# Merging the seven loads of a row's turned one-hots into one transfer in the mask stage of a graph network kernel

## The chip, the cores and the metric

The kernel runs on one core of one Trainium2 chip. The metric is device time in microseconds (us) of the whole program. Engines are TensorE (PE), VectorE (DVE), ScalarE (ACT), GpSimd (POOL) and SyncE (SP), which here only issues DMA transfers.

## What is computed

A graph network on 6,250 nodes with 64 features and 200,000 edges. The first layer adds up neighbours; the second makes three hops, in each of which every edge gets a mask from a small network of its two ends, and the messages are summed with these masks.

```python
def _L0_gnn_ref(feat, src, dst, n_nodes):
    return jax.ops.segment_sum(feat[src], dst, num_segments=n_nodes)

def _L1_gnn_ref(features, nb_W, nb_b, self_W, self_b, att1_W, att1_b, att2_W, att2_b, row, col):
    x = out = features
    for l in range(3):
        f1 = jax.nn.relu(x[row] @ nb_W[l] + nb_b[l])
        f2 = jax.nn.relu(x[col] @ self_W[l] + self_b[l])
        h = jax.nn.relu(jnp.concatenate([f1, f2], axis=1) @ att1_W[l] + att1_b[l])
        log_alpha = (h @ att2_W[l] + att2_b[l])[:, 0]
        mask = jnp.clip(jax.nn.sigmoid(log_alpha) * (1.05 + 0.45) - 0.45, 0.0, 1.0)
        rowsum = jax.ops.segment_sum(mask, row, num_segments=n) + 1e-06
        d_inv_sqrt = jnp.clip(rowsum ** (-0.5), 0.0, 10.0)
        vals = mask * d_inv_sqrt[row] * d_inv_sqrt[col]
        x = jax.ops.segment_sum(vals[:, None] * x[col], row, num_segments=n)
        out = out + x
    return out

h = relu(layernorm(x));  x = x + _L0_gnn_ref(h, src, dst, 6250)
h = relu(layernorm(x));  x = x + _L1_gnn_ref(h, ..., src, dst)
```

## The kernel before

The nodes are padded to 49 blocks of 128. The edges are sorted once into 49 x 49 bins, one for each pair of a source block and a destination block, with up to 128 edges in each. For every bin a stage called `build_and_sum` makes one-hot matrices of 128 x 128 bytes: the source one-hot turned, the destination one-hot turned, and the source one-hot as it is. They are written to `hot_scratch` in device memory, laid out as [49 rows, 128 partitions, 7 groups, 3 kinds, 7 x 128]. A "row of bins" is the 49 bins of one source block; it is worked on in NG = 7 groups of G = 7 bins.

After that, three layers run in a hardware loop. Each layer has small matrix products (`node_products`), the mask stage (`edge_masks`), the row scales (`scale_rows`) and the message stage (`sum_messages`). Both large stages read the one-hots back from `hot_scratch`, row by row.

The change lies in the mask stage. `each_row` runs row 0 unrolled and then 24 turns of a hardware loop with two rows in each (the odd row in buffer 1, the even row in buffer 0), so each buffer is used by every second row. In a row:

- SP loads `hotT_a`, the two turned one-hots, line 1089, in seven transfers of 128 x 1792 bytes (224 KB), and then `hot_a`, the unturned one, line 1091, in one transfer of 128 x 7 x 896 bytes (784 KB). Both are double buffered. Before piece g it waits until the gather of group g of the row two before is over (`gathered`), and before `hot_a` it waits until the mask sums of the row two before are over (`summed`).
- TensorE's `gather`, line 1110, makes 42 matmuls of 128x128 by 128x64 for each group: the turned source one-hot by `rows_a`, this row's node products, and the turned destination one-hot by `table`, each in three bf16 parts, into `pre_ps[g]`. Before group g it waits for piece g, and for VectorE to have emptied `pre_ps[g]` (`weigh`). After the gather of group 5 it runs `sum_masks` of the row before, line 1122, 49 matmuls of `hot_a` by `parts`, and then the gather of group 6.
- VectorE applies the relu and the attention weights (line 1190) and reduces to one logit for each edge (line 1177). ScalarE makes the sigmoid (line 1138) and copies the next row's `rows_a` (line 1144). GpSimd clips and splits the masks (lines 1156 to 1163).

The order on each engine is the order of the code; engines meet at semaphores alone. `wait_count` is a wait for a count held in a register, and it also bumps a counter (`hold_waits`, line 53).

## Time and profile before

| | us |
|---|---|
| median of 3 runs | 4841.93 |
| lowest and highest | 4841.65, 4844.85 |
| profiled execution | 4840.7 |
| its span, first to last instruction | 4839.1 |
| TensorE busy | 4293.3 (89%) |
| VectorE busy | 4118.9 (85%) |

The profile is of one execution. A row of the grouped instructions reads: line, engine, operation, output and inputs with shapes, how many, then busy time in us and mean ns of one, then the idle time of the engine just before them and what ended it. "issue" is time in which the engine waited for nothing that the profile shows. "Landing" is the time from the issue of a transfer to its last completion. The mask stages of the three layers run from about 1645 to 2155 us, 2723 to 3232 us and 3801 to 4310 us of the span.

### The profile page before, as it was taken

The numbers are of one execution on the slowest core, as the hardware profiler recorded it, in microseconds if no ns is written. First come the engines' busy times: TensorE is split into PE (matmuls) and PEld (weight loads), VectorE is DVE, ScalarE is ACT, GpSimd is POOL, SyncE is SP. The second block draws the span as 40 slices with busy tenths as digits, with TensorE's granted clock in tenths as the row PEclk, the third lists the DMA queues.
The fourth block names the chain that finished last, engine by engine and source line by source line (L and its number), as shares of the span: only waits on it lengthen the run. The fifth ranks groups of instructions, "written<-read, shape, count | busy, mean of one in ns | idle before, by whom it ended". The sixth has DMA issues, their size and how long they took to land. (4 is left out here: it accounts for less than half of the span.)

```text
span 4839.1 us, 255754 instructions
## 1 busy us (share of the span) xinstructions
PE 4293.3 (89%) x100368; PEld 4029.1 (83%) x100369; DVE 4118.9 (85%) x7921; ACT 2222.8 (46%) x3957; POOL 2223.9 (46%) x3431
## 2 busy tenths in 40 slices
PE   6888885999998699979999799979998899979998
PEld 5777774888887599978888699978888699978887
DVE  7677767999999588879999588879999588879998
ACT  0000002999999111117777211117777211127776
POOL 1222222777775222217777322227777222227776
PEclk7777776999999799989999899989999899989999
DMA  1000002888887277756665377756665477756664
GB/s 27 1 1 1 1 1 64 260 268 266 266 270 233 92 242 239 239 172 175 161 161 148 116 239 239 239 180 162 161 161 133 135 239 239 239 175 161 162 161 132
DMA packets 532160, 793.98 MB, mean 164 GB/s; under 512 B 66422, under 2 KB 466218, under 8 KB 532074
## 3 DMA queue, kind: packets, MB, share of 16 engines
q1 hardware_dynamic: 499146, 714.06, 46.8%
q0 software_dynamic: 32928, 78.72, 7.0%
q8 instruction: 60, 0.98, 0.1%
q14 instruction: 26, 0.21, 0.0%
HBM read 672.34 MB, written 120.23 MB: 164 GB/s over the span
## 5 line engine op out<-in xcount | busy, mean ns | idle before, releaser
L1110 PE MATMUL pre_ps<-rows_a,hotT_a 128*128 128x64 bf16 x21609 | 1285.5, 194 | 54.0 <-DMA hotT_a<-hot_scratch 27.3
L1339 POOL TENSOR_TENSOR message<-message,message_parts 128x448 f32<-128x448 f32 x1029 | 1100.8, 1070 | 438.4 <-ACT message_parts L1324 433.8
L1110 PE MATMUL pre_ps<-table,hotT_a 128*128 128x64 bf16 x21609 | 1286.5, 194 | 11.6 <-issue 11.6
L1110 PEld LDWEIGHTS pre_ps<-rows_a,hotT_a 128*128 128x128 fp8e4 x21609 | 1131.9, 99 | 68.1 <-issue 67.9
L1110 PEld LDWEIGHTS pre_ps<-table,hotT_a 128*128 128x128 fp8e4 x21609 | 1132.8, 99 | 5.7 <-issue 5.7
L1350 DVE TENSOR_TENSOR message_parts<-message,message_parts 128x448 bf16<-128x448 f32 x1029 | 942.3, 916 | 2.7 <-ACT message_parts L1315 2.7
L1190 DVE SCALAR_TENSOR_TENSOR weighed<-pre_ps,w 128x448 f32<-128x448 f32 x1029 | 642.4, 624 | 321.3 <-PE pre_ps L1110 229.1
L1277 PE MATMUL row_ps<-table,hot_b 128*128 128x64 bf16 x21609 | 801.3, 194 | 68.7 <-DMA hot_b<-hot_scratch 65.0
L1290 PE MATMUL sum_ps<-message_parts,hot_b 128*128 128x192 bf16 x7203 | 760.3, 245 | 90.1 <-DVE message_parts L1350 75.9
L1277 PEld LDWEIGHTS row_ps<-table,hot_b 128*128 128x128 fp8e4 x21609 | 754.9, 99 | 81.4 <-issue 81.4
L1324 ACT ACTIVATE message_parts<-message 128x448 bf16<-128x448 f32 x1029 | 593.6, 577 | 421.1 <-DVE message L1365 421.1
L1290 PEld LDWEIGHTS sum_ps<-message_parts,hot_b 128*128 128x128 fp8e4 x7203 | 556.1, 97 | 168.3 <-issue 107.1
L737 POOL DMA_DIRECT2D places<-slots_scratch x686 | 543.0, 793 | 239.0 <-issue 158.4
L1365 DVE TENSOR_TENSOR message<-row_ps,mask 128x448 f32<-128x448 f32 x1029 | 627.5, 610 | 17.0 <-PE row_ps L1277 16.7
L1177 DVE TENSOR_REDUCE logit<-weighed 128x7 f32<-128x448 f32 x1029 | 626.4, 609 | 0.0
L1138 ACT ACTIVATE gate<-logit,b 128x49 f32<-128x49 f32 x147 | 49.6, 337 | 1227.8 <-DVE logit L1177 1227.8
L1315 ACT ACTIVATE message_parts<-message 128x448 bf16<-128x448 f32 x1029 | 578.9, 563 | 1.5 <-POOL message L1339 1.3
L1158 POOL TENSOR_SCALAR fresh<-gate 128x49 f32<-128x49 f32 x147 | 35.1, 239 | 1126.9 <-ACT gate L1138 1126.9
L867 DVE TENSOR_SCALAR hot<-places,pcol 128x1792 uint8<-128x1792 uint8 x343 | 409.7, 1195 | 1.3 <-DMA places<-slots_scratch 1.2
L409 PE MATMUL bins_ps<-spread,value_w 128*98 128x128 bf16 x1764 | 317.5, 371 | 98.7 <-issue 50.5
L409 PEld LDWEIGHTS bins_ps<-spread,value_w 128*98 128x98 bf16 x1764 | 309.9, 268 | 109.4 <-issue 109.4
L831 ACT ACTIVATE hot<-src_ps 128x896 uint8<-128x896 f32 x343 | 369.3, 1077 | 43.4 <-PE src_ps L763 43.0
(145 smaller groups left out, 5554.9 us busy)
## 6 DMA issues: line engine op xcount, KB each, us to landing
hotT_a<-hot_scratch SPq DMA_DIRECT2D x1029, 224.0 KB, 4.6
hot_b<-hot_scratch SPq DMA_DIRECT2D x1029, 224.0 KB, 2.6
hot_scratch<-hot SPq DMA_DIRECT2D x343, 336.0 KB, 5.6
hot_a<-hot_scratch SPq DMA_DIRECT2D x147, 784.0 KB, 5.1
places<-slots_scratch POOLq DMA_DIRECT2D x686, 112.0 KB, 5.3
out<-res SPq DMA_DIRECT2D x1, 1536.0 KB
slots_scratch<-bins SPq DMA_DIRECT2D x49, 12.2 KB
raw<-in_src SPq DMA_DIRECT2D x1, 768.0 KB
```

The lines of the kernel that those rows point to most:

```text
L409: last = nc.tensor.matmul(bins_ps[b][:, :], value[:, b, :, w], spread[:, w, :], start=w == 0, stop=w == WIN - 1)
L737: pool.dma_start(places[:, g, e, :], tile.rearrange("r c e -> (r c e)").partition_broadcast(P))\
L1110: last = nc.tensor.matmul(pre_ps[g][:, j, :], hotT[:, b, g, end, j * P:(j + 1) * P].bitcast(FP8), table, start=end + part == 0, stop=end = ...
L1177: dve.tensor_reduce(logit[:, b, g * G:(g + 1) * G], weighed[:, (b + g) % 2, :, :], X, ALU.add)\
L1190: dve.scalar_tensor_tensor(weighed[:, (b + g) % 2, :, :], pre_ps[g][:, 0:G, :], 0.0, k.w3[:, :].unsqueeze(1).to_broadcast([P, G, D]), ALU. ...
L1277: last = nc.tensor.matmul(row_ps[g % 4][:, j, :], hot[:, b, g, 0, j * P:(j + 1) * P].bitcast(FP8), k.table_d[:, g * G + j, part, :], start ...
L1290: last = nc.tensor.matmul(sum_ps[b][:, :], hot[:, b, g, 1, j * P:(j + 1) * P].bitcast(FP8), parts[:, g, j, :, :].rearrange("p c d -> p (c ...
L1315: nc.scalar.activation(parts[:, g, :, 1, :], message[:, g, :, :], ACT.Copy)\
L1324: nc.scalar.activation(parts[:, g, :, 0, :], message[:, g, :, :], ACT.Copy)\
L1339: pool.tensor_tensor(message[:, g, :, :], message[:, g, :, :], parts[:, g, :, 0, :], ALU.subtract).then_inc(s["rest_ready"], 1)
L1350: dve.tensor_tensor(parts[:, g, :, 2, :], message[:, g, :, :], parts[:, g, :, 1, :], ALU.subtract).then_inc(s["third_ready"], 1)
L1365: dve.tensor_tensor(message[:, g, :, :], row_ps[g % 4][:, 0:G, :], k.mask[:, bass.ds(r * NB + g * G, G)].unsqueeze(2).to_broadcast([P, G, D]),
```

## The change

In the mask stage the seven transfers of `hotT_a` for a row become one transfer of 128 x 7 x 1792 bytes (1,568 KB), with one semaphore for each of the two buffers in place of seven. SP waits before it for all seven gathers of the row two before, and TensorE waits for it before the first gather of a row only.

```diff
-        sems = " ".join([f"in{b}_{g}" for b in range(2) for g in range(NG)] + ["src_in0", "src_in1"])
+        sems = "in0 in1 src_in0 src_in1"
...
-            loaded = [[s[f"in{b}_{g}"] for g in range(NG)] for b in range(2)]
+            loaded = [s["in0"], s["in1"]]
...
                     tiles = k.hot_dram[bass.ds(r, 1), :, :, :, :].rearrange("r p g a b -> (r p) g a b")
-                    for g in range(NG):
-                        if not first:
-
-                            wait_count(sp, s, s["gathered"], (r - 1) * NG + g + 1)
-                        sp.dma_start(hotT[:, b, g, :, :], tiles[:, g, 0:2, :]).then_inc(loaded[b][g], 16)
+                    if not first:
+                        wait_count(sp, s, s["gathered"], r * NG)
+                    sp.dma_start(hotT[:, b, :, :, :], tiles[:, :, 0:2, :]).then_inc(loaded[b], 16)
                     wait_count(sp, s, s["summed"], r + 1)
                     sp.dma_start(hot[:, b, :, :], tiles[:, :, 2, :]).then_inc(src_loaded[b], 16)
...
                 def gather(q, r, g, b, nth):
-                    pe.wait_ge(loaded[b][g], nth * 16)
+                    if g == 0:
+                        pe.wait_ge(loaded[b], nth * 16)
                     pe.wait_ge(s["weigh"], q + 1)
```

`gathered` starts at NG, so the value r * NG is reached when group 6 of row r - 2 is done.

SP's order in the loop's second row (even rows, buffer 0), with the wait for `gathered` on a register instruction and the DMA behind it. Before:

```order
L1091 DMA hot_a<-hot_scratch 128x7x896
L58 ISA
L1089 REGISTER_ALU [waits gathered]
L1089 DMA hotT_a<-hot_scratch 128x1792
L58 REGISTER_ALU
...
L1089 DMA hotT_a<-hot_scratch 128x1792
L58 REGISTER_ALU
L1091 REGISTER_ALU [waits summed]
L1091 DMA hot_a<-hot_scratch 128x7x896
```

The same place after (the file is one or two lines shorter, so line numbers move):

```order
L1089 DMA hot_a<-hot_scratch 128x7x896
L58 REGISTER_ALU
L1087 REGISTER_ALU [waits gathered]
L1087 DMA hotT_a<-hot_scratch 128x7x1792
L58 REGISTER_ALU
L1089 REGISTER_ALU [waits summed]
L1089 DMA hot_a<-hot_scratch 128x7x896
L102 REGISTER_ALU
```

Between the same two `hot_a` transfers, seven pairs of a wait and a transfer have become one pair.

TensorE's order at the head of the loop, where the first gather of an odd row begins. Before:

```order
L102 UNCONDITIONAL_BRANCH
L102 ISA
L1101 ISA [waits in1_0]
L1103 REGISTER_ALU [waits weigh]
L1110 MATMUL pre_ps<-rows_a,hotT_a 128x64 [waits rows_ready]
```

After:

```order
L102 UNCONDITIONAL_BRANCH
L102 ISA
L1100 ISA [waits in1]
L1102 REGISTER_ALU [waits weigh]
L1109 MATMUL pre_ps<-rows_a,hotT_a 128x64 [waits rows_ready]
```

The instructions are the same; the wait is for the whole row's transfer in place of its first piece. The order of VectorE, ScalarE and GpSimd is unchanged.

## Rows read from the trace of the kernel before

**Rows 1.** The page's part 1: busy us and share of each engine.

```profile
PE 4293.3 (89%) x100368; PEld 4029.1 (83%) x100369; DVE 4118.9 (85%) x7921; ACT 2222.8 (46%) x3957; POOL 2223.9 (46%) x3431
```

**Rows 2.** The page's part 5, then the list of waits: mask stage's gather.

```profile
L1110 PE MATMUL pre_ps<-table,hotT_a 128*128 128x64 bf16 x21609 | 1286.5, 194 | 11.6 <-issue 11.6
L1110 PE MATMUL pre_ps<-rows_a,hotT_a 128*128 128x64 bf16 x21609 | 1285.5, 194 | 54.0 <-DMA hotT_a<-hot_scratch 27.3 <-issue 26.7
...
PE pre_ps L1110 <- DMA hotT_a<-hot_scratch: 27.3, 3, 9.1
```

**Rows 3.** Busy time by window, mid-stage in the second layer; columns in the first line.

```profile
core 0: us, PE busy (x) PEld busy (x) DVE busy (x) ACT busy (x) POOL busy (x), PEclk, DMA share, GB/s
2750.00:3220.00 470.00, 461.58 (x16005) 459.31 (x16002) 378.30 (x700) 88.99 (x139) 101.05 (x373) 1.00 0.71 238
```

**Rows 4.** Timeline (start us, us, what) of TensorE where three successive rows begin.

```profile
1727.54 0.22 PE L1110 MATMUL pre_ps<-rows_a,hotT_a 128*128 128x64 bf16 x2 [0.28 <-issue]
...
1737.35 0.25 PE L1110 MATMUL pre_ps<-rows_a,hotT_a 128*128 128x64 bf16 x3
...
1747.55 0.25 PE L1110 MATMUL pre_ps<-rows_a,hotT_a 128*128 128x64 bf16 x3 [0.24 <-issue]
```

**Rows 5.** Timeline of SP's issues in one row of bins.

```profile
1726.24 0.56 SPq L1091 DMA_DIRECT2D hot_a<-hot_scratch  x1
1727.16 4.16 SPq L1089 DMA_DIRECT2D hotT_a<-hot_scratch  x7
```

**Rows 6.** The seventh of these pieces: its issue, and us to landing.

```profile
L1089 SPq DMA_DIRECT2D hotT_a<-hot_scratch x1: 333/333/333, 1731.0 to 1731.0; - x1
...
DMA to landing us min/median/max: 4.4/4.4/4.4
```

**Rows 7.** Us to landing of hot_a, 44 issues of steady rows, first layer.

```profile
DMA to landing us min/median/max: 4.8/5.1/5.4
```

**Rows 8.** By window (columns as in rows 3), one steady row of bins.

```profile
1727.00:1728.00 1.00, 0.72 (x26) 0.63 (x22) 0.70 (x2) 0.00 (x0) 0.00 (x0) 1.00 0.27 27
1728.00:1729.00 1.00, 1.00 (x41) 1.00 (x38) 0.55 (x3) 0.00 (x0) 0.00 (x0) 1.00 0.74 220
1729.00:1730.00 1.00, 1.00 (x41) 1.00 (x38) 1.00 (x2) 0.00 (x0) 0.00 (x0) 1.00 1.07 375
...
1734.00:1735.00 1.00, 1.00 (x42) 1.00 (x38) 0.94 (x2) 0.00 (x0) 0.00 (x0) 1.00 0.71 258
```

**Rows 9.** Timeline: the first issue and TensorE's first matmul, first layer.

```profile
1644.59 3.19 SPq L1089 DMA_DIRECT2D hotT_a<-hot_scratch  x7
...
1647.31 0.27 PE L1110 MATMUL pre_ps<-rows_a,hotT_a 128*128 128x64 bf16 x2 [9.12 <-DMA hotT_a<-hot_scratch]
```

**Rows 10.** First seven pieces, layers one and two: issues, and us to landing.

```profile
L1089 SPq DMA_DIRECT2D hotT_a<-hot_scratch x7: 345/433/435, 1644.6 to 1647.3; - x7
...
DMA to landing us min/median/max: 2.6/4.1/4.7
...
L1089 SPq DMA_DIRECT2D hotT_a<-hot_scratch x7: 342/428/435, 2722.7 to 2725.5; - x7
...
DMA to landing us min/median/max: 2.5/3.9/5.1
```

**Rows 11.** By window (columns as in rows 3), the first layer's start.

```profile
1647.00:1648.00 1.00, 0.69 (x14) 0.72 (x15) 0.00 (x0) 0.96 (x1) 0.00 (x0) 0.50 0.87 186
1648.00:1652.00 4.00, 4.00 (x80) 4.00 (x78) 0.64 (x2) 0.00 (x0) 0.00 (x0) 0.51 0.98 339
```

**Rows 12.** Timeline of TensorE at the loop's first entry in each layer.

```profile
1660.43 0.25 PE L1110 MATMUL pre_ps<-rows_a,hotT_a 128*128 128x64 bf16 x3 [2.31 <-issue]
...
2738.57 0.25 PE L1110 MATMUL pre_ps<-rows_a,hotT_a 128*128 128x64 bf16 x3 [2.03 <-issue]
...
3818.48 0.25 PE L1110 MATMUL pre_ps<-rows_a,hotT_a 128*128 128x64 bf16 x3 [2.85 <-issue]
```

**Rows 13.** By window (columns as in rows 3), behind the third of these.

```profile
3819.00:3823.00 4.00, 4.00 (x90) 4.00 (x87) 1.73 (x4) 0.59 (x2) 1.06 (x4) 0.57 0.47 169
```

## The prediction

> **What bounds the kernel now.** Read the page's first part before anything else: TensorE has matmuls under way for 89% of the span [rows 1]. Then the grouped instructions: the mask stage's gather, line 1110, holds 2,572 us of that as two groups of 21,609 matmuls, and the whole idle time before them is 65.6 us, of which 27.3 us is put down to the transfers that the change merges [rows 2]. The list of waits says where those 27.3 us lie: three waits, the longest 9.1 us [rows 2]. There are three layers, so each wait is the first gather of a layer's mask stage, when nothing is loaded yet. In all the other 144 rows of bins the gather never waits for a transfer.
>
> Next the steady part of the stage. Over 470 us in the middle of the second layer's stage TensorE is busy 461.6 us at full clock, VectorE 378.3, and the DMA engines 71% [rows 3]. Two rows of bins, from one return of the loop to the next, take 1747.55 - 1727.54 = 20.0 us, so 10.0 us each [rows 4]. What TensorE waits for at the return is "issue", 0.24 to 0.28 us, not data. So the stage is TensorE's, and a transfer matters only if it lands after the gather that reads it could begin.
>
> **Steady state: what is given up and what hides it.** The order of SP's instructions shows three edits: seven transfers of 224 KB become one of 1,568 KB; it waits for the end of the last gather of the row two before, where the first of the seven waited for that row's first gather; and the gather's later six groups have no wait for data. In fact SP stands in front of the `summed` wait until the mask sums of the row before, which come after group 5, so the seven are issued late already. In the trace the 784 KB of `hot_a` go out at 1726.24 and the seven at 1727.16 and after [rows 5]. The new wait ends when group 6 ends. The first matmul of the next row starts at 1727.54 after a pause of 0.28 us [rows 4], so group 6 was over at about 1727.26, and the merged transfer is issued at about 1727.3 to 1727.4: 0.2 us later than the first piece. It is issued 3.6 us earlier than the seventh piece, which goes out at 1731.0 and lands 4.4 us later, at 1735.4 [rows 6].
>
> All this data is for the row that begins at 1737.35, 9.8 us after 1727.54 [rows 4]. The merged transfer stands behind `hot_a`, which lands some 5.1 us after its issue [rows 5, 7], at 1731.3. From 1729 on the engines move 375 GB/s, and in the last us before 1735 they run out of work (258 GB/s, share 0.71) [rows 8]: they are full of work and the issue is not what holds them. So the bytes end where they ended. I take a landing at 1735.4 + 0.2 = 1735.6 and a margin of 1.8 us. **Steady cost: 0.** TensorE was not held by the waits that vanish either: they ride on register instructions that the sequencer still runs, since the order keeps their number, and both `pre_ps` groups together show only 38.3 us of "issue" in 147 rows [rows 2]. I take 0 for them. If the cover were gone, each us beyond it would cost half a us a row, because the merged transfer for one row starts at the end of the row two before: two rows would then last the transfer plus one row.
>
> A page of the Trainium skill speaks for the change at this place: "DMA: Bandwidth & Descriptors", Measured, asks for transfers of at least 1 MiB to reach 75% of peak. The trace doesn't bear it out for this queue: 224 KB pieces queued back to back already move 375 GB/s [rows 8], and by that rule too the steady term would be 0, since the bytes are hidden.
>
> **The start of each layer: the term that decides.** Here there is no cover. In the first layer SP issues the first piece at 1644.59 and TensorE starts at 1647.31, having waited 9.12 us [rows 9]. The piece took 2.6 us, 2.5 in the second layer [rows 10]. Afterwards TensorE needs all seven pieces. When is the whole there?
> - Upper bound, from the seven pieces as they are. The seventh goes out at 1647.3 and the longest of the seven takes 4.7 us: 1652.0, or 7.4 us after the first issue. In the second layer 2725.5 + 5.1 - 2722.7 = 7.9 us [rows 10].
> - Lower bound: the first piece's 2.6 us, and then six more at the steady pace. 1,568 KB are 1.606 MB, which at 375 GB/s [rows 8] take 4.3 us, or 0.6 us a piece: 2.6 + 3.6 = 6.2 us.
> - Nearest row for a single large transfer: `hot_a`, 784 KB, one DMA of the same form on the same queue, idle before it: 4.8 to 5.4 us, median 5.1 [rows 7]. The second 784 KB add 2.1 us at 375 GB/s: 7.2 us.
>
> The seven pieces have a dip on the way, 186 GB/s from 1647 to 1648 [rows 11], which a single transfer may or may not show. I take 7.0 us. TensorE then starts 7.0 - 2.6 = 4.4 us later in each layer, and three layers make **+13.2 us**, with 3 x 3.6 = 10.8 and 3 x 5.3 = 15.9 as ends. Nothing later gives it back: the stage is TensorE's, so its end moves by what its start moves. The first row's matmuls run at half clock, level 1.2 GHz, from 1647.31 until almost 1652 (granted clock 0.50, then 0.51 as a mean to 1652) [rows 11], and VectorE, ScalarE and GpSimd wait for them.
>
> The page "DMA: Bandwidth & Descriptors", Anatomy of one DMA, gives a fit made on another issuing path, 2.0 us plus bytes over 436 GB/s. As an estimate it makes the whole 5.7 us and the piece 2.5 us, so 3.2 us a layer and 9.5 us in all; the trace agrees on the piece (2.6 us) and not on the rate (375 GB/s) [rows 8, 10].
>
> **What comes back in the next few rows of bins.** At the first entry into the loop TensorE stands still for "issue": 2.31, 2.03 and 2.85 us before its first matmul [rows 12]. With the start later, the four transfers of the first two rows, 4.8 MB or 12.8 us at 375 GB/s, are through when the first row ends, some 7.0 + 10.8 us after the first issue. If all three waits fell to the shortest, 1.1 us would come back. In the third layer the longest of them is followed by four us at a mean clock of 0.57 [rows 13], so 3.4 us at half clock, which cost 1.7 us; I give that an even chance to go, 0.8 us. How long the half clock lasts after a later start is not in the trace; I take no change, and a us a layer either way for the range. Sum: **-1.9 us**, between -5 and +2. The saving on SP, six issues of 0.33 us a row, lies on a queue that next waits for TensorE's mask sums, from 1731.3 to the next `hot_a`, so 0. The reset of twelve fewer semaphores at the stage's end is one instruction as before: 0.
>
> **The sum.** 13.2 - 1.9 = +11.3 us. The profiled execution took 4840.7 us around a span of 4839.1, so it becomes 4852.0. The median of the runs is 1.2 us above it, 4841.9, which gives **4853.2 us**, 0.23% slower. About 0.2%, 9.7 us, is what a measurement of this kernel can tell from no change, so the forecast lies just beyond the line.
>
> **Rivals.**
> 1. *The large transfer flows without the dip.* The whole lands 6.2 us after issue, the start costs 10.8 us, and the loop entries give back 4 or 5: +6 us, 4848 us, not slower by the bound. For it: the seven pieces pay seven issues of some 0.43 us each [rows 10], and a single DMA pays one. Against it: `hot_a`, which is a single DMA, needs 5.1 us for half the bytes [rows 7]. It decides below 6.5 us for the whole: 3 x (6.5 - 2.6) - 1.9 = 9.8. The skill's fit above falls on this side: 9.5 - 1.9 = +8 us.
> 2. *The cover in the steady state is too thin.* The place is each row's first gather. If the merged transfer needed twice `hot_a`'s time, 10.2 us from 1727.4, it would land at 1737.6, 0.25 us after its row should start. Half of that a row, by the chain above, is 144 x 0.125 = 18 us, with the 11.3 about 4871 us. Against it: `hot_a`'s 5.1 us has a slow first us (27 GB/s, then 220) [rows 8] that isn't repeated behind a full queue. It decides from a landing 1.8 us later than I take.
> 3. *Something shortens the steady row.* If the 0.26 us of "issue" at the loop's return fell away, 23 returns in each of three layers would give 18 us: 11.3 - 18 = -7, 4835 us; with the start and the loop entries at their low ends too, 10.8 - 5 - 18 = -12, 4830 us, which would count as faster. Against it: the instructions at the loop's head are the same ones in the same order, and the wait that stands there stays.
>
> **How the numbers follow.** Forecast as summed, whole transfer 6.5 to 8 us: 0.57. Rival 1: 0.32. Rival 2: 0.07. Rival 3: 0.04. The range reaches from rival 1's low end, 10.8 - 5 - 1, to the forecast's high end, 15.9 + 2: 4846.5 to 4860. It leaves out rivals 2 and 3 and a little of the tails. Slower by over 0.2%: 0.57 + 0.07, less a little where the loop entries give back more than I take, 0.60. Within 0.2%: 0.37. Faster: 0.03.
>
> **What would show it.** Right: the wait for `hotT_a` at the start of each layer grows from 9.1 to some 13.5 us, the three waits together from 27.3 to 40; the first issue to the landing is about 7 us; two steady rows still take 20.0 us; no later gather waits for `hotT_a`. Wrong: waits for `hotT_a` counted by the hundred (rival 2), waits at the start under 13.0 us each (rival 1), or a steady pair of rows that isn't 20.0 us. A changed count or length of half-clock stretches in the first 40 us of a layer would move the sum by 1 to 2 us each.

## The result, and the profile after

| | before, us | after, us |
|---|---|---|
| median of 9 runs | 4841.65 | 4856.64 |
| lowest and highest | 4838.1, 4845.56 | 4851.9, 4863.34 |
| span of the profiled execution | 4839.1 | 4855.0 |
| TensorE busy | 4293.3 | 4294.9 |

The changed kernel is slower by 0.31%: ratio 1.0031, 95% interval 1.0021 to 1.0042, or 15 us with an interval of 10 to 20. The forecast was 4853.2 us in a range of 4846.5 to 4860. TensorE's busy time has grown by no more than 1.6 us, so nearly all of the loss is idle time between its matmuls.

The first view is the page of the changed kernel, parts 1, 5 and 6, with the lines that answer to [rows 1, 2], and from the list of waits the line on `hotT_a`:

```profile
PE 4294.9 (88%) x100368; PEld 4028.2 (83%) x100369; DVE 4120.0 (85%) x7921; ACT 2222.7 (46%) x3957; POOL 2227.7 (46%) x3431
...
L1109 PE MATMUL pre_ps<-rows_a,hotT_a 128*128 128x64 bf16 x21609 | 1286.7, 193 | 66.9 <-DMA hotT_a<-hot_scratch 43.7
...
hotT_a<-hot_scratch SPq DMA_DIRECT2D x147, 1568.0 KB, 9.0
...
PE pre_ps L1109 <- DMA hotT_a<-hot_scratch: 43.7, 8, 14.2
```

The waits for `hotT_a` grew from 27.3 us in three waits to 43.7 us in eight. Three of them are the starts of the layers. In the timeline of TensorE, kernel after, they are these, against 9.12 us in [rows 9]:

```profile
1648.89 0.26 PE L1109 MATMUL pre_ps<-rows_a,hotT_a 128*128 128x64 bf16 x2 [14.16 <-DMA hotT_a<-hot_scratch]
...
2734.31 0.27 PE L1109 MATMUL pre_ps<-rows_a,hotT_a 128*128 128x64 bf16 x2 [13.68 <-DMA hotT_a<-hot_scratch]
...
3819.66 0.26 PE L1109 MATMUL pre_ps<-rows_a,hotT_a 128*128 128x64 bf16 x2 [13.57 <-DMA hotT_a<-hot_scratch]
```

They add up to 41.4 us. The other five waits hold the remaining 2.3 us. The first is the transfer itself. SP's issues at the first layer's start, and the answer for the tile `hotT_a` there, kernel after:

```profile
1641.14 0.62 SPq L1087 DMA_DIRECT2D hotT_a<-hot_scratch  x1
1641.82 0.65 SPq L1089 DMA_DIRECT2D hot_a<-hot_scratch  x1
...
L1087 SPq DMA_DIRECT2D hotT_a<-hot_scratch x1: 624/624/624, 1641.1 to 1641.1; - x1
...
DMA to landing us min/median/max: 7.6/7.6/7.6
```

The whole of a row lands 7.6 us after its issue, where 7.0 was assumed, and TensorE starts 1648.89 - 1641.14 = 7.75 us after the issue. Before it was 2.72 us [rows 9].

Next the steady rows. SP's issues in the row that [rows 5] shows, the landing of the transfer issued at 1727.29, and the landings of 43 issues in the middle of the first layer's stage:

```profile
1726.05 0.54 SPq L1089 DMA_DIRECT2D hot_a<-hot_scratch  x1
1727.29 0.54 SPq L1087 DMA_DIRECT2D hotT_a<-hot_scratch  x1
...
DMA to landing us min/median/max: 9.0/9.0/9.0
...
L1087 SPq DMA_DIRECT2D hotT_a<-hot_scratch x43: 542/543/570, 1707.2 to 2128.9; - x43
...
DMA to landing us min/median/max: 8.5/8.9/10.0
```

And TensorE's rows of bins, as in [rows 4]:

```profile
1727.35 0.22 PE L1109 MATMUL pre_ps<-rows_a,hotT_a 128*128 128x64 bf16 x2 [0.28 <-issue]
...
1737.15 0.22 PE L1109 MATMUL pre_ps<-rows_a,hotT_a 128*128 128x64 bf16 x2
...
1747.36 0.22 PE L1109 MATMUL pre_ps<-rows_a,hotT_a 128*128 128x64 bf16 x2 [0.23 <-issue]
```

A pair of rows still takes 1747.36 - 1727.35 = 20.0 us. But the data for the row that starts at 1737.15 landed at 1727.29 + 9.0 = 1736.3, only 0.86 us before it, where the prediction had 1.8 us. The landings scatter from 8.5 to 10.0 us, so some come too late. Over the 138 rows from row 3 on in the three layers, worked out from the single landings, the median time from the last landing to the row's first matmul is 1.84 us before and 0.83 us after.

Where did the bytes lose time? Busy time by window in that row (columns as in [rows 3]); the last two figures of a line are the DMA share and GB/s:

```profile
1729.00:1730.00 1.00, 1.00 (x41) 1.00 (x37) 0.92 (x2) 0.04 (x1) 0.00 (x0) 1.00 1.06 371
1730.00:1731.00 1.00, 1.00 (x41) 1.00 (x38) 0.95 (x2) 0.55 (x2) 0.43 (x2) 1.00 0.91 275
...
1734.00:1735.00 1.00, 1.00 (x42) 1.00 (x39) 1.00 (x2) 0.00 (x0) 0.00 (x0) 1.00 0.68 256
1735.00:1736.00 1.00, 1.00 (x46) 1.00 (x43) 0.88 (x3) 0.00 (x0) 0.00 (x0) 1.00 0.15 56
```

There is a dip to 275 GB/s from 1730 to 1731, and a thin tail, 56 GB/s from 1735 to 1736. The completions of the single transfer explain the tail: it is done when the last of the 16 DMA engines is, and in the trace their completions lie between 1734.67 and 1736.29, 1.6 us apart. Those of the seventh piece before lay between 1734.95 and 1735.42, 0.5 us apart. Over the same 138 rows the median spread is 1.7 us after (0.8 to 3.3) and 0.7 us for the seventh piece before (0.4 to 2.4).

### The profile page after: what moved, and what is told of

Read it like the earlier page. It is cut to its first block and busy times, and to the rows that moved or that the text cites. A ratio compares the mean times of both kernels' runs of the same rounds, so it can differ in the third digit from the quotient of the medians.

```text
span 4855.0 us, 251416 instructions
## 1 busy us (share of the span) xinstructions
PE 4294.9 (88%) x100368; PEld 4028.2 (83%) x100369; DVE 4120.0 (85%) x7921; ACT 2222.7 (46%) x3957; POOL 2227.7 (46%) x3431
## 5 line engine op out<-in xcount | busy, mean ns | idle before, releaser
L1109 PE MATMUL pre_ps<-rows_a,hotT_a 128*128 128x64 bf16 x21609 | 1286.7, 193 | 66.9 <-DMA hotT_a<-hot_scratch 43.7
L1109 PE MATMUL pre_ps<-table,hotT_a 128*128 128x64 bf16 x21609 | 1287.8, 193 | 11.7 <-issue 11.7
L409 PEld LDWEIGHTS bins_ps<-spread,value_w 128*98 128x98 bf16 x1764 | 309.9, 268 | 111.4 <-issue 111.4
```

The lines of the kernel that those rows point to most:

```text
L409: last = nc.tensor.matmul(bins_ps[b][:, :], value[:, b, :, w], spread[:, w, :], start=w == 0, stop=w == WIN - 1)
L1109: last = nc.tensor.matmul(pre_ps[g][:, j, :], hotT[:, b, g, end, j * P:(j + 1) * P].bitcast(FP8), table, start=end + part == 0, stop=end = ...
```

## Where the 15.9 us of the two spans went

The table is worked out from the starts of single matmuls in the two traces; the stretches of the three layers are added up. "Start" is from the first issue of `hotT_a` to the first gather matmul. A row of bins lasts from its first gather matmul to the next row's first. Rows 3 to 47 are split into those that end inside the loop's turn (69) and those that end at its return (66).

| stretch, us | before | after | difference |
|---|---|---|---|
| start | 8.10 | 22.18 | +14.1 |
| rows 0 to 2 | 117.6 | 114.1 | -3.5 |
| rows 3 to 47, ending inside the turn | 676.5 | 678.5 | +2.0 |
| rows 3 to 47, ending at the return | 675.7 | 677.6 | +1.9 |
| until the first issue, and from one layer's messages to the next layer's first issue | 1754.7 | 1757.2 | +2.5 |
| message stage and the rest | | | -1.0 |

In this bookkeeping of one execution the start is nearly the whole difference, as predicted, and three other terms are of 2.5 to 4 us each, with different signs. That it would go if the start alone were undone doesn't follow; the experiments below test it. The +2.5 is itself the sum of two differences: the first issue comes 3.5 us earlier after than before, and the two stretches between layers are 6.0 us longer together.

**The first rows are shorter, above all at the loop's first entry.** In the timeline of TensorE, kernel after, the rows that answer to [rows 12] are:

```profile
1660.76 0.22 PE L1109 MATMUL pre_ps<-rows_a,hotT_a 128*128 128x64 bf16 x2
...
2745.81 0.22 PE L1109 MATMUL pre_ps<-rows_a,hotT_a 128*128 128x64 bf16 x2
...
3831.47 0.19 PE L1109 MATMUL pre_ps<-rows_a,hotT_a 128*128 128x64 bf16 x1 [0.39 <-issue]
```

Waits of 2.31, 2.03 and 2.85 us for "issue" have become 0.39 us or less. In exchange there is a wait earlier, in row 0, and the one that row 2 had before is longer (from start to start of two matmuls 2.8, 3.4 and 2.8 us in the three layers, before 2.5, 2.5 and 1.7). The longest of each kind in TensorE's timeline, kernel after:

```profile
1656.80 0.26 PE L1109 MATMUL pre_ps<-rows_a,hotT_a 128*128 128x64 bf16 x3 [1.28 <-issue]
...
2765.46 0.21 PE L1109 MATMUL pre_ps<-table,hotT_a 128*128 128x64 bf16 x1 [3.16 <-issue]
```

The list of queues for the stretch of the second of these, 2762 to 2766, shows what else was moving:

```profile
DMA  7899889999999999998998989989765442322222
...
q1 hardware_dynamic: 690, 1.22, 82.1%
q8 instruction: 1, 0.02, 1.5%
```

In these four us there is one packet on the instruction queue, among 690 packets of the one-hots on engines that are some nine tenths busy for the first seven tenths of the stretch. My reading is that TensorE stands for its code behind data.

The start times of the single packets on that queue, 16 KB each, bear this out. At all 42 loop entries of the 14 profiles (those of the runs below included) the last such packet goes out 2.7 to 3.1 us before row 1's first matmul, whether TensorE idles 0.1 or 3.1 us there. What differs is how far it lies behind the packet ahead of it: 6.0, 5.5 and 6.4 us before, where TensorE idles 2.31, 2.03 and 2.85 us; 3.7, 3.5 and 3.9 us after, where it idles 0.11, 0.11 and 0.39. Over the 42 entries the idle time goes with that distance almost in step (correlation 0.99), and from row 5 to row 47 of each layer before there is no packet on that queue. What spaces the packets out is still an inference: no run here moved the code alone.

**A second half-clock stretch takes a part of it back.** The long waits of row 2 are followed by half clock in all three layers after, and not before. By window (columns as in [rows 3]), four us from the matmul that ends the longest wait of row 2, the three layers after, then the second layer before:

```profile
1679.85:1683.85 4.00, 4.00 (x87) 4.00 (x87) 2.02 (x4) 0.00 (x0) 0.00 (x0) 0.59 0.11 39
2765.46:2769.46 4.00, 4.00 (x90) 4.00 (x90) 2.03 (x4) 0.00 (x0) 0.00 (x0) 0.61 0.11 38
3850.02:3854.02 4.00, 4.00 (x85) 4.00 (x85) 2.30 (x4) 0.00 (x0) 0.00 (x0) 0.57 0.11 40
...
2758.49:2762.49 4.00, 3.96 (x137) 3.90 (x137) 3.18 (x6) 0.00 (x0) 0.00 (x0) 1.00 0.19 67
```

A mean of 0.57 to 0.61 over four us means 3.1 to 3.4 us at half clock (1.2 GHz), which do the work of half that time at full clock: an estimate of 1.6 to 1.7 us lost in each layer, some 5 us in all. Before, the only such stretch past row 0 is the one behind the third loop entry [rows 13]. In the second profile of the kernel after (below) row 2 has it in two of the layers (0.62 and 0.57).

**The stretch between the layers varies in length.** From the last message matmul of a layer to the first issue of the next layer's mask stage, by window, before and then after (the clock is third from the end):

```profile
2667.85:2722.71 54.86, 36.83 (x176) 22.27 (x174) 25.26 (x55) 16.35 (x27) 25.64 (x14) 0.79 0.03 4
...
2668.61:2727.04 58.43, 39.48 (x177) 23.62 (x174) 25.27 (x55) 16.34 (x27) 25.63 (x14) 0.77 0.02 4
```

The work is the same to within three records; VectorE, ScalarE and GpSimd are busy for the same time, and TensorE is busy for 2.7 us more at a lower mean granted clock. The change touches nothing there. In the profiles of before, after and the eight runs below that load row 0 within the mask stage, the 20 such stretches are of 54.9 to 58.7 us, nine of them under 56. Runs that merge all rows have short ones too (54.9 us in the second profile of the kernel after), but before was profiled once, with two short ones. I take these us for chance in a profile; that the change has no part in them is argued, not shown.

## Experiments

The claims to be told apart: the loss comes from the start, where TensorE waits for the whole instead of one piece; or it comes from the other 48 rows, where the cover is too thin; and, for the cause, the size of the transfer or the coarser wait. Runs with the same time of before in the table at the end ran on one chip, beside the same runs of before.

**Row 0 in pieces, the other rows merged.** Against the kernel after:

```diff
-                    if not first:
+                    if first:
+                        for g in range(NG):
+                            sp.dma_start(hotT[:, b, g, :, :], tiles[:, g, 0:2, :]).then_inc(pieces[g], 16)
+                    else:
                         wait_count(sp, s, s["gathered"], r * NG)
-                    sp.dma_start(hotT[:, b, :, :, :], tiles[:, :, 0:2, :]).then_inc(loaded[b], 16)
+                        sp.dma_start(hotT[:, b, :, :, :], tiles[:, :, 0:2, :]).then_inc(loaded[b], 16)
...
-                    if g == 0:
-                        pe.wait_ge(loaded[b], nth * 16)
+                    if first:
+                        pe.wait_ge(pieces[g], 16)
+                    elif g == 0:
+                        pe.wait_ge(loaded[b], nth * 16 if b == 1 else (nth - 1) * 16)
```

> The merged kernel with one part undone: the first row of each layer is loaded in seven pieces again, each with its own wait; the 144 other rows keep the merged transfer and its single wait. Theory (the start is the whole cost): TensorE starts 2.7 us after the first issue in each layer instead of 7.2 to 7.8, so 5.0 + 4.6 + 4.4 = 14 us go, and the kernel lands within 0.1% of the kernel before, 4840 to 4846 us. Rival (the merged transfer costs in the steady rows, where it lands 9.0 us after its issue with some 0.8 us to spare): no more than half of the 15 us goes, 4849 us or more.

Measured: 4862.94 us, ratio 1.0041 (1.0027 to 1.0055). The start is back at 8.1 us for the three layers, and yet the kernel is 21.6 us slower than before. The trace says that 9.0 us stand in the rows that end at the loop's return: median 10.36 us each, where before has 10.25 and after 10.21. Another 8.9 us stand in rows 0 to 2 (126.5 us against 117.6). Here are two loop returns of this kernel; the idle time is 0.39 us against 0.24 to 0.28 in [rows 4]:

```profile
1727.37 0.22 PE L1115 MATMUL pre_ps<-rows_a,hotT_a 128*128 128x64 bf16 x2 [0.39 <-issue]
...
1747.53 0.19 PE L1115 MATMUL pre_ps<-rows_a,hotT_a 128*128 128x64 bf16 x1 [0.39 <-issue]
```

The count `(nth - 1) * 16` was mine and no part of the change. So the run doesn't answer its question.

**Seven transfers, one wait.** Against after:

```diff
-                    sp.dma_start(hotT[:, b, :, :, :], tiles[:, :, 0:2, :]).then_inc(loaded[b], 16)
+                    for g in range(NG):
+                        sp.dma_start(hotT[:, b, g, :, :], tiles[:, g, 0:2, :]).then_inc(loaded[b], 16)
...
-                        pe.wait_ge(loaded[b], nth * 16)
+                        pe.wait_ge(loaded[b], nth * (16 * NG))
```

> Waits as in the merged kernel (one for the whole row, SP after the last gather, TensorE before the first), but seven transfers of 224 KB in place of one of 1,568 KB, on one semaphore for each buffer. Theory (it is the coarser wait, not the size of the transfer, that costs): the start is as late as the seventh piece of the kernel before, 7.4 to 7.9 us after the first issue, so the time stays at 4853 to 4860 us. Rival (a large transfer is itself slower to land): the start is nearer 6.2 us and the time 4850 or less. On the steady landing: issued from 1727.3 on at 0.64 us each, the seventh piece goes out 3.8 us later and lands 4.4 us after that, 8.2 us after the first issue, against 9.0 us for the one transfer; if the size is what makes the landing late, the occasional late rows (five waits beside the three starts) vanish.

Measured: 4856.45 us, ratio 1.0032 (1.0021 to 1.0043). The changed count costs here too (median 10.34 us at the return, 6.6 us in all), so the total says little. The parts of the trace say more. In the list of waits of this kernel:

```profile
PE pre_ps L1110 <- DMA hotT_a<-hot_scratch: 43.0, 3, 14.6
```

Three waits, all at starts, which take 8.19, 8.10 and 7.48 us from the first issue: as late as with the single transfer (7.75, 7.27, 7.16). It is the wait for the whole that costs at the start, not the size of the transfer. No later row waits for `hotT_a`. In rows 3 to 48 the last of the seven pieces lands a median 8.0 us after the first issue, where the single transfer takes 9.0, and 1.92 us before its row begins (after: 0.83). The longer returns, 0.13 us each, don't explain that, so it is the size that makes the steady landings late.

**Row 0 merged, the others in seven.** Against before:

```diff
-                    for g in range(NG):
-                        if not first:
-
+                    if first:
+                        sp.dma_start(hotT[:, b, :, :, :], tiles[:, :, 0:2, :]).then_inc(s["row0_in"], 16)
+                    else:
+                        for g in range(NG):
                             wait_count(sp, s, s["gathered"], (r - 1) * NG + g + 1)
-                        sp.dma_start(hotT[:, b, g, :, :], tiles[:, g, 0:2, :]).then_inc(loaded[b][g], 16)
+                            sp.dma_start(hotT[:, b, g, :, :], tiles[:, g, 0:2, :]).then_inc(loaded[b][g], 16)
...
-                    pe.wait_ge(loaded[b][g], nth * 16)
+                    if not first:
+                        pe.wait_ge(loaded[b][g], nth * 16 if b == 1 else (nth - 1) * 16)
+                    elif g == 0:
+                        pe.wait_ge(s["row0_in"], 16)
```

> The kernel before with one part of the change alone: row 0 of each layer is loaded in one transfer with one wait, all other rows keep seven pieces with seven waits. Theory (start alone): +13 to +15 us, 4854 to 4857 us, and no wait for hotT_a beside the three at the starts. Rival (steady rows pay part of it): under +8 us.

Measured: 4859.42 us, ratio 1.0037 (1.0024 to 1.0051), with 8.0 us more than before in the rows at the loop's return (median 10.36 us). Confounded in the same way.

**Row 0 loaded a stage earlier, the others in seven.** Against before; `hotT_a` is allocated over both stages, and the stage ahead loads row 0 into it behind its weights and waits for it at its end:

```diff
+                sp.dma_start(k.hotT[:, 0, :, :, :],
+                             k.hot_dram[0:1, :, :, 0:2, :].rearrange("r p g a b -> (r p) g a b")).then_inc(s["row0_in"], 16)
+                sp.wait_ge(s["row0_in"], 16)
...
-                    pe.wait_ge(loaded[b][g], nth * 16)
+                    if not first:
+                        pe.wait_ge(loaded[b][g], nth * 16 if b == 1 else (nth - 1) * 16)
```

> The kernel before, with row 0's 1,568 KB loaded during the small matrix products ahead of the mask stage, one transfer behind the weights, so that the first gather waits for no transfer. Theory (the path at a layer's start runs through the issue and landing of row 0): TensorE starts some 2.4 us earlier in each layer, bounded below by ScalarE's copy of rows_a, which ends at 1646.7 against TensorE's start at 1647.3; so at least 0.6 x 3 = 2 us and at most 7 us faster, 4835 to 4840 us. Rival (the transfer disturbs the matrix products or their weight loads): no gain or a loss of a few us.

Measured: 4840.73 us, ratio 1.0001 (0.9992 to 1.001). Of the gain at the start 9.6 us go to the loop's return (685.36 us against 675.72).

**The same with the counts left alone.** The four following runs keep `nth * 16` as it is. Where row 0 is loaded apart, SP adds the 16 itself, as in this piece of the first of them:

```diff
                     if first:
                         for g in range(NG):
                             sp.dma_start(hotT[:, b, g, :, :], tiles[:, g, 0:2, :]).then_inc(pieces[g], 16)
+                        sp.sem_inc(loaded[b], 16)
...
-                        pe.wait_ge(loaded[b], nth * 16 if b == 1 else (nth - 1) * 16)
+                        pe.wait_ge(loaded[b], nth * 16)
```

Row 0 in pieces, the others merged:

> Row 0 in seven pieces and all other rows merged, as in the first form of this experiment, which landed at 4862.9 us. In that form the wait of the even rows compared with a changed count, and the trace shows 0.15 us more at each of the 69 returns of the loop, 10 us in all. Here SyncE adds the missing 16 to the merged semaphore itself, so TensorE's loop is the same as in the merged kernel. Theory (the start is the cost, the head of the loop was the disturbance): the returns take 10.21 us a row again, the start 2.7 us a layer, and the time is 4840 to 4848 us. Rival (pieces first and merged transfers after slow down the first three rows of a layer, 126.5 us there against 114.1 merged): 4850 to 4856 us.

Measured: 4851.7 us, ratio 1.0026 (1.0017 to 1.0035): the rival's range, not the 4840 to 4848 of the theory. Row 0 merged, the others in seven:

> The kernel before with row 0 alone merged, in the same clean form (TensorE's loop as in the kernel before). Its first form came to 4859.4 us, of which the returns of the loop explain 8 us. Theory: the start costs 14 us, the first three rows give back 3 to 6, so 4849 to 4853 us, the returns 10.21 to 10.25 us. Rival (the head of the loop does not matter): 4857 or more again.

Measured: 4852.61 us, ratio 1.0024 (1.0015 to 1.0033). Row 0 a stage earlier, the others in seven:

> The kernel before with row 0 loaded during the small matrix products, TensorE's loop unchanged. The first form (a changed count in the even rows) took 4840.7 us with returns of 10.39 us in place of 10.25: 9 us lost there. Theory: those 9 us come back, 4830 to 4834 us, faster than the kernel before by 0.15 to 0.25%. Rival: no change, 4839 or more.

Measured: 4830.72 us, ratio 0.9981 (0.9972 to 0.999). Row 0 a stage earlier, the others merged:

> The merged kernel with row 0 loaded during the small matrix products, TensorE's loop unchanged. It takes the start away and leaves what the merged transfer costs in the other rows. Theory (start 22.2 us in three layers is the main cost, late rows 4 us the rest): 4836 to 4842 us, that is 2 to 8 us above the same kernel with seven pieces. Rival (the merged transfer costs nothing in the steady rows): equal to the kernel with seven pieces within 2 us.

Measured: 4847.19 us, ratio 1.0012 (1.0003 to 1.0021). Both expectations for this run are missed: 4836 to 4842 us, and within 2 us of the kernel above it. In all four the median row at the loop's return is back at 10.21 us. A loop return of the first of the four shows it:

```profile
1726.81 0.22 PE L1116 MATMUL pre_ps<-rows_a,hotT_a 128*128 128x64 bf16 x2 [0.23 <-issue]
```

That settles where the extra 9 us of the first runs came from. The instructions listed at the head of the loop are the same in both forms; in the trace the step from the loop's register operation to the wait is 0.37 us in the first form and 0.26 us in the kernel after. What the sequencer does in between isn't recorded.

Now the medians, each against the before of the same chip (4840.05 us):

| us | others in seven | others merged | difference |
|---|---|---|---|
| row 0 in pieces | 4840.05 (before) | 4851.7 | +11.7 |
| row 0 merged | 4852.61 | 4854.75 (another chip, before 4839.83) | +2.1 |
| row 0 a stage earlier | 4830.72 | 4847.19 | +16.5 |

The start alone costs 12.6 us. But merging the other 48 rows costs 12 to 16 us where the mask stage starts early, and about 2 us where it starts late. The two parts don't add: 12.6 + 11.7 would be 24.3, the change costs 15. Read the other way: each part alone costs most of the 15 us, and undoing one of them in the changed kernel gives back only 2 to 3 (4854.75 to 4852.61 or to 4851.7). The intervals are some 4 us wide to either side, so the sizes are rough, but the difference between +2.1 and +16.5 is beyond them.

The traces show part of the reason in rows 0 to 2 of the three layers: 117.6 us before, 112.1 with only row 0 merged, 111.4 in a second profile of the kernel after (114.1 in the first), but 120.8 with row 0 in pieces and the others merged, and 117.1 and 123.1 for the two that load row 0 early. With an early start these rows run beside 4.8 MB of transfers, and merged ones lengthen them by 3.2 (120.8 - 117.6) and 5.9 us (123.1 - 117.1); with a late start the queue is drained when the loop is entered, and they get shorter. Late steady rows add 0 to 7 us by the profiles: rows 3 to 47 are 0.4 us shorter than before in the first of the four, and 7.3 us longer in the last than in the third. That doesn't fill the 11.7 us of the first of the four. Its span is 8.5 us above before's, of which 3.2 lie in rows 0 to 2, and 6.5 ahead of and between the stages, where the kernels don't differ and the lengths vary in all of them. These parts are a guide only: the profiled execution of the first of the four took 4849.21 us against a median of 4851.7, and that of the last was the slowest of its eleven, 4853.61 against 4847.19. Why merging the other rows costs 12 to 16 us with an early start stays open.

**More bytes ahead of the merged transfer.** Against after, with one tile more; its data is read by nobody, so 448 KB a row (with `0:4` in place of `0:2`, 896 KB) are only load:

```diff
                     if not first:
                         wait_count(sp, s, s["gathered"], r * NG)
+                        wait_count(sp, s, more_in[b], nth * 16 if b == 1 else (nth - 1) * 16)
+                        sp.dma_start(more[:, b, :, :, :], tiles[:, 0:2, 0:2, :]).then_inc(more_in[b], 16)
```

> The merged kernel with 448 KB more loaded ahead of each row's merged transfer, into a buffer that nothing reads. It measures how thin the cover in the steady rows is. In the merged kernel's trace the transfer lands 8.9 us after its issue and the row that reads it starts 9.67 or 9.82 us after that issue, of which some 0.3 us pass between a landing and a first matmul that waited for it. Theory (0.4 to 0.6 us of cover, then half a us a row for each us beyond): the landing moves by 448 KB at 375 GB/s, 1.2 us, so 0.7 us too late and 0.35 us a row, 144 rows make 50 us on top of the merged kernel: 4890 to 4915 us, waits for hotT_a in over 100 rows. Rival (the cover is 1.8 us, as predicted): no change, 4860 us at most.

Measured: 4886.66 us, ratio 1.0095 (1.008 to 1.0111), 32 us above the unchanged merged kernel on the same chip, where 4890 to 4915 was expected.

> The same with 896 KB more, 2.4 us of transfer. Theory (half a us a row for each us beyond the cover): 1.9 us too late, 0.95 us a row, 137 us on top of the merged kernel, 4980 to 5010 us. Rival (every us beyond the cover costs a whole us a row, since each row has one transfer): some 270 us, 5100 us or more.

Measured: 5056.97 us (one run), 202 us above it, between the two ranges that were expected. The list of waits, first the kernel with 448 KB, then that with 896 KB:

```profile
PE pre_ps L1118 <- DMA hotT_a<-hot_scratch: 74.7, 45, 14.4
...
PE pre_ps L1118 <- DMA hotT_a<-hot_scratch: 178.7, 77, 14.3
```

The 8 waits of the kernel after have become 45, and then 77, which is about every second of the 144 rows: two rows share one late transfer, as the prediction's chain says. With 448 KB the waits grow by 31.0 us, which is about the loss of that run. These bytes would take 1.2 us at 375 GB/s (0.459 MB), but in the trace the landing moves by less: counted from the start of the row before, its median goes from 9.2 to 9.7 us. The engines move 315 GB/s from 1727 to 1737, where they moved 241 in the kernel after. So half a us more is already enough to use up the margin of many rows, which the prediction put at 1.8 us. With 896 KB the waits grow by 135 us, and the rest has another cause; the page's part 1 of that kernel:

```profile
PE 4368.9 (86%) x100368; PEld 4102.5 (81%) x100369; DVE 4119.9 (81%) x7921; ACT 2222.0 (44%) x3957; POOL 2220.9 (44%) x3431
```

TensorE, which now pauses in every second row, is busy for 74 us more with the same matmuls, and its mean granted clock over the span is 0.913 against 0.926. In rows 3 to 47 of its three mask stages the mean granted clock is 0.94 to 0.96, against 1.00 in the kernel after. In the second layer, for instance, the row that starts at 3006.56 behind a wait of 2.04 us lasts 11.36 us at a mean of 0.85, where a row without a pause takes 9.81. So these pauses cost themselves, and matmuls behind them run at a lower clock as well.

**The change once more.** The kernel after, on the chip of the last two and of the next.

> The merged kernel once more, unchanged, in the same stretch of chip time as the others, for a second profile of it. Theory: 4853 to 4860 us; the wait at the start of each layer 13.5 to 14.5 us; some late rows beside the three starts, though not the same ones. If the late rows do not come again, they were a chance of one execution.

Measured: 4854.75 us, ratio 1.0033 (1.0021 to 1.0045). Its trace has a start of 22.3 us and seven waits for `hotT_a`, 43.4 us; rows 3 to 47 are 1.5 us longer than before's (1.5 inside the turn, 0.0 at the return), where the first profile had 3.8. So the starts repeat, and the late rows are few and vary.

**Row 0 of both large stages a stage earlier.** Against before: as in the third of the four, and the same for `hot_b` of the message stage, loaded in `scale_rows`:

```diff
+        @block.sync
+        def _(sp):
+            sp.dma_start(k.hotB[:, 0, :, :, :],
+                         k.hot_dram[0:1, :, :, 1:3, :].rearrange("r p g a b -> (r p) g a b")).then_inc(s["row0_in"], 16)
+            sp.wait_ge(s["row0_in"], 16)
```

> The kernel before with row 0 of both large stages loaded ahead of time: the mask stage's during the small matrix products (this alone came to 4830.7 us), and the message stage's during the row scales, while the DMA queue is idle. Theory: the message stage of each layer starts up to 2.7 us earlier (its first issue to TensorE's start in the trace), less the time that the start needs without a transfer, some 0.3 us, so 5 to 7 us less than 4830.7: 4823 to 4827 us. Rival (the first rows of the message stage lose it again to the half clock and the loop's first entry): 4828 or more.

Measured: 4827.91 us, ratio 0.9974 (0.9964 to 0.9984): 11.9 us below before and some 27 below after, the fastest kernel of the study, though 0.9 us above the range expected. In its trace a layer is at least 2.1 us shorter between row 48 of the mask stage and the last message matmul (527.9 us, before 530.0 to 531.3). The gain over the kernel with the mask stage's row alone, 2.6 us in the two differences from before, is within the intervals.

Expected is the range of the theory, as it was put down ahead of each run; four of the twelve were met.

| run | expected, us | median, us | ratio, 95% interval | before, us |
|---|---|---|---|---|
| after | 4846.5 to 4860 (range) | 4856.64 | 1.0031, 1.0021 to 1.0042 | 4841.65 |
| row 0 in pieces, changed count | 4840 to 4846 | 4862.94 | 1.0041, 1.0027 to 1.0055 | 4841.33 |
| seven transfers, one wait | 4853 to 4860 | 4856.45 | 1.0032, 1.0021 to 1.0043 | 4841.33 |
| row 0 merged, changed count | 4854 to 4857 | 4859.42 | 1.0037, 1.0024 to 1.0051 | 4841.33 |
| row 0 earlier, changed count | 4835 to 4840 | 4840.73 | 1.0001, 0.9992 to 1.001 | 4841.33 |
| row 0 in pieces, others merged | 4840 to 4848 | 4851.7 | 1.0026, 1.0017 to 1.0035 | 4840.05 |
| row 0 merged, others in seven | 4849 to 4853 | 4852.61 | 1.0024, 1.0015 to 1.0033 | 4840.05 |
| row 0 earlier, others in seven | 4830 to 4834 | 4830.72 | 0.9981, 0.9972 to 0.999 | 4840.05 |
| row 0 earlier, others merged | 4836 to 4842 | 4847.19 | 1.0012, 1.0003 to 1.0021 | 4840.05 |
| 448 KB more a row | 4890 to 4915 | 4886.66 | 1.0095, 1.008 to 1.0111 | 4839.83 |
| 896 KB more a row | 4980 to 5010 | 5056.97 | one run | 4839.83 |
| after once more | 4853 to 4860 | 4854.75 | 1.0033, 1.0021 to 1.0045 | 4839.83 |
| row 0 of both stages earlier | 4823 to 4827 | 4827.91 | 0.9974, 0.9964 to 0.9984 | 4839.83 |

## The prediction, step by step

- **The start, +13.2 us.** Right in mechanism and near in size: +14.1 us in the profile. The whole takes 7.6 us in the first layer, not 7.0. The run with seven transfers and one wait puts it down to the wait for the whole; the run with row 0 alone merged gives 12.6 us for it with what follows from it. "Nothing later gives it back" holds for that run, but not for the changed kernel, where undoing the start gives back only some 3 us.
- **Loop entries, -1.1 us.** Mis-sized. I let all three waits fall to the shortest seen; they fell from 7.19 us together to under 1. The reason that I gave, a drained queue, fits the traces; but with a drained queue nearly the whole wait is gone, not only its excess.
- **The row behind the third entry, -0.8 us.** It went, and more came. Row 1 of the third layer ran at a mean clock of 0.85 before and runs at 1.00 after, but in row 2 all three layers now have such a stretch, some 5 us by the estimate above. The prediction took no change of the clock and named a changed count of half-clock stretches as what would move the sum. What came back in rows 0 to 2 as a whole is 3.5 us (-1.9 predicted), or 6.2 in the second profile, because waits of 1.1 to 1.5 us (start to start) in row 0, those of about 3 us in row 2 and the half clock behind these take a part of it again.
- **Steady rows, 0 with a margin of 1.8 us.** This is the step that failed. "So the bytes end where they ended" leaves out that the consumer now waits for the slowest of 16 engines over the whole transfer: 9.0 us to landing where I had 8.3, a margin of 0.86 us, and +3.8 us from late rows (+1.5 in the second profile). One late row, kernel after, whose transfer took 10.4 us from an issue at 2993.4:

```profile
L1087 SPq DMA_DIRECT2D hotT_a<-hot_scratch x1: 543/543/543, 2993.4 to 2993.4; - x1
...
DMA to landing us min/median/max: 10.4/10.4/10.4
...
3004.12 0.25 PE L1109 MATMUL pre_ps<-rows_a,hotT_a 128*128 128x64 bf16 x3 [0.77 <-DVE weighed L1189]
```

  The data was there at 3003.8 and the row began at 3004.12. The wait is put down to VectorE, but the landing is what came just ahead of it. So the list of waits, with 2.3 us in five waits behind the starts, doesn't hold all of these 3.8.
- **Rival 1, the transfer flows without the dip.** It needed a landing under 6.5 us; it was 7.6. False.
- **Rival 2, the cover too thin.** Its price was right in kind: with 448 KB more a row it is the whole loss. It was to decide 1.8 us later than the landing I took; 0.86 us is the margin in the trace. In the change itself it is there as a fringe of late rows.
- **Rival 3, a shorter steady row.** The pair of rows is 20.0 us before and after. False for the change; the changed counts showed that the same place can cost 0.15 us a return.
- **What the sum left out.** That start and steady rows are not independent. In the profile the sum of +11.3 is 4.6 us short of 15.9: +0.9 at the start, -1.6 in the first rows, +3.8 in the late rows, +2.5 of chance between the stages, -1.0 in the message stage and the rest. The median came 3.4 us above the forecast. That it came so near is in part luck. Measured apart, the start costs 12.6 us and the other rows 11.7 us, where the sum had 13.2 and 0; only because the two overlap is the whole 15 and not 24. A small slip besides: the low end of the range, 10.8 - 5 - 1 = 4.8 us, leads to 4846.7 and not to 4846.5, which changes nothing.

On the size of transfers the Trainium skill, "DMA: Bandwidth & Descriptors", Measured, asks for at least 1 MiB, beside a table measured on another issuing path. The rows above speak for the opposite here: 1,568 KB in one transfer land later than the same bytes in seven queued ones, 1736.3 against 1735.4, on a queue that moved 375 GB/s with the small ones [rows 8].

## What to carry to other kernels

A transfer that is split so that its consumer can start on the first piece must be costed at the stage's cold start, times the number of starts, before anyone counts the issues saved: here 4.7 us in each of three layers, and nothing in the steady rows to pay for it. Costs found for two parts of a change, each alone, need not add: here each costs about 12 us and both together 15. Give the landing of a merged transfer a margin of more than a us over the sum of its bytes, since it lands with its slowest engine. If a cold start shows up as a wait in the profile, load the first tile one stage earlier: that was worth 9 us here with one stage and 12 with two, with the seven pieces kept; with merged transfers the kernel stayed 7 us slower than before.

## What the runs showed of the hardware

- TensorE idles 0.1 to 3.1 us at the loop's first entry. It is 2.0 to 2.9 us before, where 300 GB/s and more still move in the last three us, and 0.1 to 0.4 us after, where under 15 GB/s do. The last 16 KB packet of the instruction queue goes out 2.7 to 3.1 us ahead in every case, and the idle time follows its distance from the packet before it, 3.5 to 6.6 us (42 entries, correlation 0.99). With row 0 early and the others merged the idle time is 1.2 to 2.6 us though the queue moves only 45 to 65 GB/s in the last three us, so the state of the queue at the entry itself doesn't tell.
- Behind a wait of 2.6 to 3.2 us in row 2 the granted clock is half for some 3 us (mean 0.57 to 0.61 over four us); behind one of 2.71 us in row 1 of the second layer before it stayed at 1.00.
- A changed expression in a wait's count, with the same listed instructions at the loop's head, lengthened the returns by some 0.15 us (medians of 10.34 to 10.39 us against 10.21 to 10.25), 6.6 to 9.6 us in the kernel.
- Completions of a 1,568 KB transfer on the 16 engines lay a median 1.7 us apart (0.8 to 3.3), those of the seventh 224 KB piece 0.7 us (0.4 to 2.4), over 138 rows each.
- The stretch between two layers takes 54.9 to 58.7 us with the same work; the mean granted clock was 0.79 in one of 54.86 us and 0.77 in one of 58.43 us.
